# Three PSUM banks for key-major attention products, one for values, and a group's first transposition moved behind its values

## What is computed

```python
h = layernorm(x)                                   # over the 256 channels, no scale or shift
q, k, v = rope(h @ Wq.T), rope(h @ Wk.T), h @ Wv.T # rope before the split into heads
att = softmax(q k.T / sqrt(16))                    # per head: 512 x 512
x = x + (att v) @ Wu.T + bu

h = layernorm(x)
prev = concat([0, h[:, :-1]])                      # the token before
xr, xk = mu_r*h + (1-mu_r)*prev, mu_k*h + (1-mu_k)*prev
x = x + sigmoid(xr @ W_r.T) * (square(relu(xk @ W_k.T)) @ W_v.T)
```

## Time and profile before

| what | value |
|---|---|
| median of 3 runs | 2408.97 us (2403.08 to 2410.29) |
| the profiled execution | 2414.42 us |
| its span in the trace | 2412.6 us |
| mean granted TensorE clock | 0.958 of 2.4 GHz |
| busy share of PE, DVE, ACT, POOL | 93%, 84%, 68%, 58% |

### The profile page before, as it was taken

One profiled execution on the slowest core, in us unless ns is written; L12 is line 12 of the kernel. 1 busy time (PEld: TensorE's weight loads), 2 busy tenths in 40 slices (PEclk: granted clock), 3 DMA queues, 4 the chain that ended last, 5 costly groups with the idle time before them and its releaser, 6 DMA issues.

```text
span 2412.6 us, 48257 instructions
## 1 busy us (share of the span) xinstructions
PE 2247.4 (93%) x13084; PEld 1196.5 (50%) x13084; DVE 2036.4 (84%) x3982; ACT 1644.9 (68%) x3137; POOL 1406.3 (58%) x1184
## 2 busy tenths in 40 slices
PE   5999999999999999999999999999999999999995
PEld 4445445555455455544555454455545555545433
DVE  5778888889888888888988888898889989998862
ACT  2467777767677777767767677676767767777653
POOL 5336765556666565765546765555765646676234
PEclk8789999999999999999999999999999999999977
DMA  6434445544345553344544345553344554444400
GB/s 155 108 88 97 97 89 120 124 105 99 89 87 122 123 119 93 99 101 90 122 113 99 82 93 116 123 122 88 97 104 91 122 125 101 98 92 99 92 28 22
DMA packets 133571, 243.18 MB, mean 101 GB/s; under 512 B 24848, under 2 KB 79760, under 8 KB 120976
## 3 DMA queue, kind: packets, MB, share of 16 engines
q1 hardware_dynamic: 133264, 239.56, 44.0%
HBM read 136.71 MB, written 83.89 MB: 91 GB/s over the span
## 4 chain that ended last, share of the span: by engine, by line
PE 33%; POOL 26%; issue 19%; DVE 12%; ACT 4%; SPq 3%; DMA 2%; DVEq 1%; POOLq 0%; ACTq 0%
PE d_ps L956 13%; PE st_ps L894 9%; POOL f_lo L465 6%; DVE mx L693 5%; PE pv_ps L926 5%; PE s_ps L912 4%; POOL rope_t L415 3%; POOL yn L481 2%; POOL xrT L444 2%; POOL r_lo L451 2%; POOL parts L409 2%; POOL rs L473 2%; POOL parts L425 2%; ACT probs L652 2%; POOL rope_t L418 1%
## 5 line engine op out<-in xcount | busy, mean ns | idle before, releaser
L652 ACT ACTIVATE probs<-st_ps 128x512 f32<-128x512 f32 x2048 | 1155.6, 597 | 624.2 <-PE st_ps L894 617.1
L693 DVE TENSOR_REDUCE mx<-s_ps 128x1 f32<-128x512 f32 x2048 | 1339.0, 678 | 286.0 <-PE s_ps L912 284.9
L912 PE MATMUL s_ps<-k_st,q_st 48*128 48x512 f32 x2048 | 862.6, 480 | 49.6 <-DVE mx L693 42.1
L894 PE MATMUL st_ps<-q_st,k_st 50*128 50x512 f32 x2048 | 820.5, 464 | 62.8 <-issue 30.8
L894 PEld LDWEIGHTS st_ps<-q_st,k_st 50*128 50x128 f32 x2048 | 332.9, 189 | 680.7 <-ACT probs L652 439.9
L926 PE MATMUL pv_ps<-probs,v_ext 128*32 128x512 f32 x4096 | 558.3, 617 | 0.0
L912 PEld LDWEIGHTS s_ps<-k_st,q_st 48*128 48x128 f32 x2048 | 360.3, 189 | 136.4 <-DVE mx L693 122.8
L473 POOL TENSOR_TENSOR rs<-ve,mhalf 128x2 f32<-128x2 f32 x128 | 89.7, 701 | 485.3 <-DVE mean L761 485.3
L465 POOL TENSOR_TENSOR f_lo<-yn,f_hi 128x512 fp32r<-128x512 f32 x128 | 175.0, 1377 | 83.0 <-ACT f_hi L620 83.0
L458 POOL TENSOR_TENSOR f_lo<-attnT,f_hi 128x512 fp32r<-128x512 f32 x64 | 86.2, 1347 | 203.0 <-ACT f_hi L608 202.9
L926 PEld LDWEIGHTS pv_ps<-probs,v_ext 128*32 128x32 f32 x4096 | 81.5, 109 | 167.9 <-issue 164.6
(11 more groups left out here) (118 smaller groups left out, 3988.3 us busy)
## 6 DMA issues: line engine op xcount, KB each, us to landing
parts_scratch<-parts SPq DMA_DIRECT2D x64, 1024.0 KB, 5.4
q_st<-parts_scratch SPq DMA_DIRECT2D x128, 256.0 KB, 6.0
k_st<-parts_scratch SPq DMA_DIRECT2D x128, 256.0 KB, 6.8
xn<-in_L_attn_x_dram SPq DMA_DIRECT2D x32, 512.0 KB, 8.5
q_st<-parts_scratch SPq DMA_DIRECT2D x128, 128.0 KB, 7.4
k_st<-parts_scratch SPq DMA_DIRECT2D x128, 128.0 KB, 7.1
attnT<-attn SPq DMA_DIRECT2D x512, 32.0 KB, 2.0
y<-in_L_attn_x_dram SPq DMA_DIRECT2D x32, 512.0 KB, 5.8
```

Source lines behind the costliest of these rows:

```text
L652: nc.scalar.activation(probs[:, u % SLOTS, j, :], st_ps[:, n % 2, :], ACT.Exp, scale=float(D) ** -0.5).then_inc(exp_done, 1)
L693: nc.vector.tensor_reduce(mx[:, col:col + 1], s_ps[:, n % 2, :], AX.X, ALU.max).then_inc(max_done, 1)
L894: nc.tensor.matmul(st_ps[:, n % 2, :], k_st[par][row:row + SROWS + MROWS, slot, c * P:(c + 1) * P], q_st[par][row:row + SROWS + MROWS, slo ...
L912: nc.tensor.matmul(s_ps[:, n % 2, :], q_st[at][row:row + SROWS, slot, qc * P:(qc + 1) * P], k_st[at][row:row + SROWS, slot, :], start=True ...
```

## The change

`st_ps` gets a third bank and `pv_ps` gives one up, so that PSUM's eight banks stay in use: three for key-major products, two for query-major ones, one for values, two for dense pieces.

- Key-major product n goes to bank n % 3 (the last of a step, n = 63, to bank 1), and waits for the exponential of the last product in the same bank: three back, but two back for (15,3) and for (0,1) of the next step.
- With one bank, the values of a group's first chunk wait for stage 0 of the group before, which reads the bank.
- `sums` becomes a tile of its own, so that `yT_evac` and stage 0 need not wait for each other's use of `ynT`; both waits go.
- Stage 0 moves in VectorE's table: group 0 from (7,0) to (5,0), where it is the first of two entries, group 1 from (12,0) to (9,0), group 2 from (15,0) to (13,0). Group 3 stays at (1,0). Stages 1 and 2 stay where they are.

```diff
+        sums = sb("sums", [P, T])
...
-        sums = ynT[:, 0, 1:T + 1]
...
-        st_ps = ctx.enter_context(nc.psum_tensor("st_ps", [P, 2, T], F32))
+        st_ps = ctx.enter_context(nc.psum_tensor("st_ps", [P, 3, T], F32))
...
-        pv_ps = ctx.enter_context(nc.psum_tensor("pv_ps", [P, 2, T], F32))
+        pv_ps = ctx.enter_context(nc.psum_tensor("pv_ps", [P, 1, T], F32))
...
-            return (d_ps, st_ps, s_ps, pv_ps)[w // 2][:, w % 2, :]
+            return (d_ps, st_ps, s_ps)[w // 2][:, w % 2, :] if w < 6 else st_ps[:, 2, :]
...
+        def ring_bank(n):
+
+            return 1 if n == SCORES - 1 else n % 3
+
+        def ring_last(n):
+
+            k = n - 1
+            while ring_bank(k % SCORES) != ring_bank(n):
+                k -= 1
+            return k + 1
...
                 def yT_evac(n):
...
-                        if b.has(NG, 1):
-                            act.wait_ge(attn_done, b.count(NG, 1))
...
-                            nc.scalar.activation(probs[:, u % SLOTS, j, :], st_ps[:, n % 2, :], ACT.Exp,
+                            nc.scalar.activation(probs[:, u % SLOTS, j, :], st_ps[:, ring_bank(n), :], ACT.Exp,
...
                 def normalise(s, g, stage):
...
-                        if g == 1 and s.plus(-1).has(4, 4):
-                            dve.wait_ge(shift_done, s.plus(-1).count(4, 4))
-                        nc.vector.transpose(sums, pv_ps[:, g % 2, :]).then_inc(norm_step, 1)
+                        nc.vector.transpose(sums[:, :], pv_ps[:, 0, :]).then_inc(norm_step, 1)
...
-                          (5, 0): [(stats2_of, 0, 0)], (5, 1): [(stats2_of, 0, 1)], (5, 3): [(residual, 1), (split_max, b, 2, 0)],
+                          (5, 0): [(normalise, b, 0, 0), (stats2_of, 0, 0)], (5, 1): [(stats2_of, 0, 1)], (5, 3): [(residual, 1), (split_max, b, 2, 0)],
...
-                          (7, 0): [(normalise, b, 0, 0)], (7, 1): [(normalise, b, 0, 1)],
+                          (7, 1): [(normalise, b, 0, 1)],
...
-                          (8, 3): [(stats1_of, 0, 0)], (9, 1): [(stats1_of, 0, 1)],
+                          (8, 3): [(stats1_of, 0, 0)], (9, 0): [(normalise, b, 1, 0)], (9, 1): [(stats1_of, 0, 1)],
...
-                          (12, 0): [(normalise, b, 1, 0)], (12, 1): [(normalise, b, 1, 1)],
+                          (12, 1): [(normalise, b, 1, 1)],
...
-                          (13, 2): [(split_max, nxt, 0, 0)], (13, 3): [(split_max, nxt, 0, 1)],
+                          (13, 0): [(normalise, b, 2, 0)], (13, 2): [(split_max, nxt, 0, 0)], (13, 3): [(split_max, nxt, 0, 1)],
...
-                          (15, 0): [(normalise, b, 2, 0)], (15, 1): [(normalise, b, 2, 1)],
+                          (15, 1): [(normalise, b, 2, 1)],
...
-                    if b.has(SCORES, n - 1):
-                        pe.wait_ge(exp_done, b.count(SCORES, n - 1))
-                    nc.tensor.matmul(st_ps[:, n % 2, :],
+                    if b.has(SCORES, ring_last(n)):
+                        pe.wait_ge(exp_done, b.count(SCORES, ring_last(n)))
+                    nc.tensor.matmul(st_ps[:, ring_bank(n), :],
...
-                    if c == 0 and s.has(3 * NG, 3 * g - 5):
-                        pe.wait_ge(norm_step, s.count(3 * NG, 3 * g - 5))
+                    if c == 0 and s.has(3 * NG, 3 * g - 2):
+                        pe.wait_ge(norm_step, s.count(3 * NG, 3 * g - 2))
```

More of the change, by code:

```diff
@@ L711, in normalise @@
                         return
-                    blocks = sums.rearrange("p (k r) -> p k r", r=32)
+                    blocks = sums[:, :].rearrange("p (k r) -> p k r", r=32)
                     if stage == 0:
@@ L730, in normalise @@
                             dve.wait_ge(attn_in, s.count(64 * NG, 64 * g))
-                        nc.vector.transpose(attn[:, :], sums).then_inc(attn_done, 1)
+                        nc.vector.transpose(attn[:, :], sums[:, :]).then_inc(attn_done, 1)
                 def residual(n):
@@ L842, in step @@
                           (10, 3): [(shift, 0, 0)], (11, 2): [(shift, 0, 1)],
-                          (12, 0): [(normalise, b, 1, 0)], (12, 1): [(normalise, b, 1, 1)],
+                          (12, 1): [(normalise, b, 1, 1)],
                           (12, 3): [(normalise, b, 1, 2)],
-                          (13, 2): [(split_max, nxt, 0, 0)], (13, 3): [(split_max, nxt, 0, 1)],
+                          (13, 0): [(normalise, b, 2, 0)], (13, 2): [(split_max, nxt, 0, 0)], (13, 3): [(split_max, nxt, 0, 1)],
                           (14, 1): [(stats1_of, 1, 0)], (14, 3): [(stats1_of, 1, 1)],
-                          (15, 0): [(normalise, b, 2, 0)], (15, 1): [(normalise, b, 2, 1)],
+                          (15, 1): [(normalise, b, 2, 1)],
                           (15, 3): [(normalise, b, 2, 2)]}
                 if first(b.plus(2)):
-                    extras[5, 0] = [(first_rope, 0), (first_rope, 1), (first_low, 0)]
+                    extras[5, 0] = [(normalise, b, 0, 0), (first_rope, 0), (first_rope, 1), (first_low, 0)]
                     extras[7, 3] = extras.pop((8, 3)) + extras.pop((9, 1)) + extras.pop((14, 1)) + extras.pop((14, 3))
@@ L921, in values @@
                         pe.wait_ge(v_done, s.count(2, 2))
-                    if c == 0 and s.has(3 * NG, 3 * g - 5):
-                        pe.wait_ge(norm_step, s.count(3 * NG, 3 * g - 5))
+                    if c == 0 and s.has(3 * NG, 3 * g - 2):
+                        pe.wait_ge(norm_step, s.count(3 * NG, 3 * g - 2))
                     for j in range(GH):
                         h = head_at(GH * g + j)
-                        ins = nc.tensor.matmul(pv_ps[32 * j:32 * j + 32, g % 2, :], v_ext[half][:, c, VW * h:VW * h + 32],
+                        ins = nc.tensor.matmul(pv_ps[32 * j:32 * j + 32, 0, :], v_ext[half][:, c, VW * h:VW * h + 32],
                                                probs[:, u % SLOTS, j, :], start=(c == 0), stop=(c == TC - 1))
```

## The result

| kernel | median, us | ratio of the runs to those of the kernel before, 95% interval |
|---|---|---|
| before | 2407.44 (8 runs) | 1 |
| changed | 2422.69 (8 runs) | 1.0058 [1.0035, 1.0080] |

The change makes the kernel slower by 0.58%, some 14 us. 2399 had been forecast, and the range ended at 2418. The profiled executions lie closer together than the medians: 2414.42 us before, 2417.14 changed.

What follows compares the result with a forecast made beforehand. A chain passing between VectorE (nearest to full) and TensorE was taken to pace each batch. Terms summed to −0.33 us per batch, times 30, −10 us: 2399 us against a 2409 median; range 2384 to 2418, the forecast's own 2394 to 2404.

Steps and rivals of the forecast that it cites:

- Units 5 to 8: Group 0's transposition makes Q0 0.63 us late; the third bank pays that back at (8,1), leaving (8,2) 0.15 late.
- VectorE's gap at (8,2): Sign in the changed profile: VectorE's wait at (8,2), 0.80 us before, stays about as before.
- Unit 9: Group 1's transposition at (9,0) fills VectorE's 0.64 us gap at (9,2), leaving it 0.1 late; GpSimd's lateness costs nothing.
- Units 12 and 13: Without the transposition at (12,0), (13,1) is not held by VectorE, and R0, unit 13's dense piece, comes 0.33 us earlier.
- One pv bank: In unit 9, values wait for the previous group's transposition, which ends over 0.4 us ahead: price 0.
- Rival 2: Unit 8 does not pay back: ScalarE holds its dense piece, (8,2) 0.9 us late, R0 +0.47; 2423 us, chance 0.13.
- Rival 1: The whole gap goes: (8,1) 0.5 us earlier, unit 12 adding 0.45, 29 us gained in all; 2380 us, chance 0.12.
- The sign to watch: In the changed profile, VectorE's total wait for query-major products falls some 10 us or more, its busy time unchanged.
- The sign about the clock: Forecast wrong if TensorE's longer wait before Q0 brings more 1.2 GHz stretches than the mean clock of 0.958 holds.
- The 284.9 us: VectorE's 390 waits for query-major products, 284.9 us, taken as nearly all of its idle time.
- Half of 1.03: Unit 8's dense piece: half its 1.03 us behind ScalarE's release at 1551.68 ends at 1552.25, 0.10 later than before.
- The gap at (13,2): VectorE's 0.99 us gap in unit 13 shrinks to 0.66, and group 2's transposition of 0.63 still fits.

Runs made afterwards that it cites:

- e5: Kernel of e1 with key-major products waiting for the exponential two back, as before the change: 2407.12 us, ratio 0.9992 to the kernel before.
- e1: Changed kernel with `ve` and `mean` of LN1's statistics in unit 9 each split into two one-column operations: 2397.48 us, ratio 0.9934 to the kernel before.
- e3: Kernel before with `ve` and `mean` of LN1's first half split into single columns: 2407.44 us, ratio 0.9981 to the kernel before.
- e2: Changed kernel with key-major products waiting for the exponential two back despite three banks: 2431.68 us, ratio 1.0063 to the kernel before.
- e6: Changed kernel with the edits of e1 and e4 together: 2354.14 us, ratio 0.9762 to the kernel before.
- e4: Kernel before with GpSimd's addition of bu made as two operations of half the size: 2380.78 us, ratio 0.9868 to the kernel before.

## Why the prediction was wrong

- **Units 5 to 8: right.** Q0 came +0.55 (0.63 forecast), (8,1) 0.33 behind (8,0), (8,2) +0.09; e5 shows that the third bank does it. VectorE's gap at (8,2) shrank to 0.34, where the prediction wanted it about as before: the multiplication of group 0 at (7,1) takes 1.21 in place of 0.61, held by GpSimd too, so that VectorE came +0.56 late and not +0.33. No later event shows it: (8,2) is less late than forecast.
- **Unit 9: the step that failed.** "It is now ready at 1556.44 + 0.15 + 0.63 = 1557.22 [...] The 0.64 gap is eaten, δ = +0.1." The sum moved `ve` and `mean` with their old durations. They did not keep them: `ve` starts 0.68 later and GpSimd's difference 0.54 later, and where they now meet, `ve` or `mean` is held through a difference; in one batch of three both are, one behind the other. The same paragraph saw that GpSimd's chain is 0.63 late, and gave it "no price" because VectorE wants nothing of it before its shift. δ = +0.75 at (9,2) in place of +0.1; the hold costs 53.11 − 52.20 = 0.91 us per batch in the mean (e1), × 31 = 28 us, and the ratios of e1 and the changed kernel differ by 1.24%, 30 us.
- **Units 12 and 13: right in form.** "R0 moves by what (12,2) is late, less 0.43": 0.76 less 0.43 gives +0.33, seen +0.35; in e1 R0 comes at the very −0.33.
- **One pv bank: right.** No row of TensorE's waits names the transposition, and the values follow the products as before.
- **Rival 2 gave nearly the measured time** (2423), by a mechanism that did not happen: (8,2) is 0.09 late, not 0.9, and neither norm2(1) nor qk_evac(0,1) holds it. Rival 1 is answered by e1 and e3: without the hold the change gains 11 us, not 29.
- **The sign to watch was in the text and half read.** VectorE's waits fell by 40 us, more than the 10 asked for, while its busy time did not stay: waiting had turned into longer operations. The sign about the clock did not come: the mean granted clock is 0.964 in the changed kernel's profiled execution, 0.958 before.
- **Readings that were off without deciding anything.** The 284.9 us are three quarters of the 376 us in which VectorE is not busy, not nearly all. Half of 1.03 behind 1551.68 is 1552.20, not 1552.25. The gap at (13,2) does not shrink to 0.66, since the maxima in front of it come earlier as well: 0.99 less 0.63 leaves 0.36, seen 0.40. In rival 1, −0.5 and −0.45 make −0.95.

The rows show what passed and what did not. `ve` and `mean` on 128x2, the multiplication (128x256, two inputs from SBUF) and the shift (128x512, two) did not get on while GpSimd's operation ran, and went on at its end. The maxima and transpositions from PSUM, the reciprocal (0.24 us at 1591.68, inside GpSimd's 2.37 from 1591.29) and the one-column operations ran beside it. The Trainium skill (SBUF — State Buffer, SBUF: two separate sides) says that VectorE and GpSimd share one pair of SBUF ports, that an operation of VectorE in a two-port mode or with two SBUF inputs and one of GpSimd that reads SBUF shut each other out, and that whoever starts first keeps the pair for its whole instruction. This case's trace agrees: 1.02 us for `mean` against 1.04 for the difference. The Trainium skill (VectorE: DVE Perf Modes, Mode 2×_2P) also says that the mode splits the access along the outermost dimension that is longer than one and needs it even (or odd and equal on both sides). A single column has no such dimension, and the page leaves that case open; no run here shows the mode itself, so why single columns escape is not shown.

What stays open: the stretches at 1.2 GHz. In the changed kernel and in e1 one falls into unit 2 of 7 and 6 of 12 odd batches, in before, e2 and e5 in 1, 1 and 0; units 0 to 3 then take 1.25 us more (18.58 against 17.33). The windows of one such batch of the changed kernel show it (us, busy us of PE, PEld, DVE, ACT, POOL, then the granted clock, DMA share, GB/s):

```profile
1598.00:1601.00 3.00, 2.12 (x13) 0.70 (x5) 3.00 (x4) 2.75 (x6) 2.42 (x2) 1.00 1.03 384
1601.00:1605.00 4.00, 4.00 (x21) 2.81 (x24) 2.46 (x7) 1.63 (x4) 0.00 (x0) 0.57 0.22 63
```

TensorE did 2.12 us of work in the 3 us ahead of it, while VectorE stood in group 3's multiplication until 1599.30. In e6, where that is short (0.9 us), no odd batch has such a stretch; but before, e2 and e5 have the same 2.0 us there and hardly a stretch. What causes it was not tried by itself. Nor are units 0 to 3 settled as a whole: behind an odd batch they take 20.7 us before and 19.5 in the changed kernel, behind an even one 17.3 and 18.1 (means of 12). Units 4 to 15 alone cost (53.11 − 52.56) × 31 = 17 us, and the profiled executions differ by 2.7.

## What to carry to other kernels

When work on VectorE is moved, its operations between SBUF tensors need not keep their durations: lay GpSimd's timeline beside it and ask of each such operation which GpSimd instruction runs when it arrives. Here the hold showed as a longer busy time of a small instruction, not as idle time or a wait, so compare mean durations by line before and after. What helped was a shorter GpSimd operation where VectorE waits (0.89 us in place of 2.00), and a form of VectorE's operation that is not held (the single columns of e1).

## What was not expected of the hardware

An operation on 256 numbers (128x2) can cost 1.08 us, as long as a whole 128x512 operation of GpSimd. Some hundredths of a microsecond separate the cases: `ve` passed where it came 0.21 or 0.07 ahead of the end of GpSimd's running operation; `mean`, at that end, had to wait for the next. They do not explain all: in the kernel before `mean` comes some 0.06 ahead of such an end in 26 batches, and is held in 12 of them and not in 14. So the price of a move depends on phase: 13, 28, 24 and 15 batches of 32 were hit in four kernels (before, changed, e2, e4) whose order at that place differs by one transposition or not at all.
